# First blocks of S rearranged: block 0 loaded in column halves, its x tile alone, and the low halves of blocks 1 and 2 made in front of the next block's sums

## The reference

```python
x = x + gnn(layernorm(x), adj, adj)      # x [2048, 512], adj [2048, 2048]
x = x + ffn(layernorm(x)[None], ...)[0]

def gnn(x, Coefficient2, A):             # called with Coefficient2 = A = adj
    S = (A + A.T) * 0.5 + eye
    deg = S.sum(1); dinv = where(deg > 0, deg ** -0.5, 0)
    return (Coefficient2 @ (dinv[:, None] * S * dinv[None, :])) @ x
# ffn: 8 routed experts (top 1) and a shared one, weights made ternary
```

## Time and profile before

| | us |
|---|---|
| median of 3 runs (727.76 to 730.76) | 729.55 |
| the profiled execution | 729.79 |
| its span in the profile | 728.1 |
| PE busy | 659.4 |
| DVE busy | 488.8 |
| ACT busy | 390.1 |
| POOL busy | 202.4 |
| PE's first matmul of the stage | 19.25 |
| last matmul of block 15 starts | 112.67 |

### The profile page before, as it was taken

How to read it: one execution, slowest core, us unless ns; L and a number is a source line. 1 busy time by engine, 2 the same in 40 slices (tenths; PEclk the granted TensorE clock), 3 DMA queues, 4 the chain that set the end, 5 groups by cost and what they waited for, 6 DMA issues and landing times.

```text
span 728.1 us, 16147 instructions
## 1 busy us (share of the span) xinstructions
PE 659.4 (91%) x5313; PEld 385.2 (53%) x5313; DVE 488.8 (67%) x1071; ACT 390.1 (54%) x726; POOL 202.4 (28%) x195
## 2 busy tenths in 40 slices
PE   0799998999998999999868788799999999999995
PEld 0344443444444554444424365477767676777763
DVE  4878966646674556589899868966775465555554
ACT  2667547859986765777547662223342233233331
POOL 2123310000000000077666606620020445344332
PEclk9999999999999999999998999999999999999999
DMA  8999942675887787667566785354248677677751
GB/s 350 416 420 417 417 172 58 193 185 144 228 243 243 256 271 269 234 207 226 173 240 215 226 228 147 92 164 105 86 59 203 147 211 186 179 191 176 174 148 34
DMA packets 107103, 151.68 MB, mean 208 GB/s; under 512 B 64286, under 2 KB 64286, under 8 KB 102944
## 3 DMA queue, kind: packets, MB, share of 16 engines
q1 hardware_dynamic: 91280, 117.74, 52.5%
q0 software_dynamic: 6960, 20.99, 9.7%
q10 hardware_dynamic: 8800, 12.09, 5.2%
HBM read 119.57 MB, written 19.16 MB: 191 GB/s over the span
## 4 chain that ended last, share of the span: by engine, by line
PE 60%; DVE 13%; DMA 10%; issue 7%; POOL 4%; ACT 4%; DVEq 0%; SPq 0%; ACTq 0%; POOLq 0%
PE bank L1536 14%; PE bank L1509 14%; PE bank L1375 9%; PE bank L1377 9%; PE bank L1376 9%; DMA region<-in_adj_t 5%; DMA work<-in_w 2%; PE bank L1414 2%; DVE work L1081 2%; POOL xb L578 2%; DVE xb L1127 1%; POOL xb L580 1%; ACT junk L732 1%; DVE s L1062 1%; DMA work<-in_adj_t 1%
## 5 line engine op out<-in xcount | busy, mean ns | idle before, releaser
L1536 PE MATMUL bank<-region,work 128*128 (+1 forms) x624 | 142.5, 382 | 4.2 <-DVE work L1229 4.2
L870 ACT ACTIVATE work<-work 128x512 f32<-128x512 f32 x78 | 48.5, 622 | 180.6 <-DVE work L1219 180.6
L1375 PE MATMUL bank<-zreg,work 128*128 (+1 forms) x256 | 98.2, 384 | 13.6 <-DVE work L1150 10.8
L1509 PE MATMUL bank<-zreg,region 128*128 128x128 f16 x1728 | 100.9, 219 | 0.0
L1509 PEld LDWEIGHTS bank<-zreg,region 128*128 (+1 forms) x1728 | 98.1, 98 | 4.3
L1376 PE MATMUL bank<-zreg,work 128*128 (+1 forms) x256 | 98.1, 383 | 0.0
L1377 PE MATMUL bank<-zreg,work 128*128 (+1 forms) x256 | 98.1, 383 | 0.0
L1536 PEld LDWEIGHTS bank<-region,work 128*128 128x128 f16 x624 | 59.2, 98 | 70.8 <-issue 8.9
L1375 PE MATMUL bank<-region,work 128*128 128x512 f16 (+1 forms) x192 | 74.8, 389 | 23.1 <-DVE region L994 23.1
L732 ACT ACTIVATE junk<-work 128x512 f16<-128x512 f32 x124 | 77.7, 626 | 22.8 <-DMA work<-in_w 20.7
L575 POOL TENSOR_TENSOR rb<-rb,power 128x2 f32<-128x2 f32 x16 | 17.4, 1087 | 255.5 <-DVE rb L1141 255.4
(11 more groups left out here) (158 smaller groups left out, 1009.8 us busy)
## 6 DMA issues: line engine op xcount, KB each, us to landing
work<-in_w SPq DMA_DIRECT2D x62, 512.0 KB, 4.1
region<-in_adj SPq DMA_DIRECT2D x16, 1024.0 KB, 10.8
region<-in_adj_t SPq DMA_DIRECT2D x16, 1024.0 KB, 7.5
work<-in_adj_t SPq DMA_DIRECT2D x32, 384.0 KB, 4.2
zreg<-s_scratch SPq DMA_DIRECT2D x24, 256.0 KB
xb<-in_w SPq DMA_DIRECT2D x10, 512.0 KB, 4.2
zreg<-in_x SPq DMA_DIRECT2D x4, 1024.0 KB, 9.8
h_scratch<-hb POOLq DMA_DIRECT2D x16, 256.0 KB, 3.7
```

Of the source, the lines that this page charges most:

```text
L870: nc.scalar.activation(h1[:, cols], pre[:, cols], ACT.Silu).then_inc(h1_ok, 1)
L1375: nc.tensor.matmul(dst, a_hi, b_hi, start=start, stop=False, skip_group_check=True)
L1509: last = nc.tensor.matmul(ps_h[b][f // 4][:, (f % 4) * P:(f % 4 + 1) * P], w, ht[n % RING][:, c:c + P], start=(f % 4 == 0 and d == 0 and h ...
L1536: last = nc.tensor.matmul(ps_y[b][:, :].rearrange("p (d c) -> p d c", d=DB), h1hl[:, b, h, f * P:(f + 1) * P], w, start=(f == 0 and h == 0 ...
```

## The change

Block 0's two loads are split into column halves with semaphores of their own, so that the sums of the first 1024 columns wait for the first halves alone. Tile 0 of x is a load of its own in front of block 1; tiles 1 to 3 (`x_rest`) follow block 1. In every round the next x batch is loaded one block later. On DVE the statistics, the root and the scales of tile 0 are made by themselves, the low half of S's block 0 comes in front of them, and for blocks 1 and 2 low_s, dinv_of and low_u come in front of the next block's sums. On ACT the moments of batch 1 move by one step: none after block 0.

```diff
-            load_a(0, 0, True)
-            sp.dma_start(xhat[:, 0:UNROLL, :], x_t[:, 0:UNROLL, :]).then_inc(x_in[0], 16)
+            for c in (slice(0, G0_COLS), slice(G0_COLS, N)):
+                half = first_half if c.start == 0 else first_rest
+                sp.dma_start(a_in[:, 0, c], adj_j[0, :, c]).then_inc(half, 16)
+                sp.dma_start(t_in[:, 0, c], adjt_j[0, :, c]).then_inc(half, 16)
+            sp.dma_start(xhat[:, 0:1, :], x_t[:, 0:1, :]).then_inc(x_in[0], 16)
...
             load_a(1, 1, True)
+            sp.dma_start(xhat[:, 1:UNROLL, :], x_t[:, 1:UNROLL, :]).then_inc(x_rest, 16)
+            load_a(2, 2, True)
             load_x(1)
-            for s in range(2, UNROLL):
-                load_a(s, s, True)
+            load_a(3, 3, True)
             with sp.Fori(1, NT // UNROLL - 1) as i:
                 for s in range(UNROLL):
                     load_a(UNROLL * i + s, s, False)
-                    if s == 0:
+                    if s == 1:
                         load_x(i + 1)
...
             AFTER = {0: (0, 1, 2), 1: (3,), 2: (4, 5)}
+            AFTER_FIRST = {1: (0, 1), 2: (2, 3, 4, 5)}
...
-            sums_of(0, 0)
-            dve.wait_ge(x_in[0], 16)
-            for s in range(UNROLL):
-                x_stats(0, s)
-            x_first()
-            dinv_of(0, 0)
-            x_scales(0, True)
-            stream_round(0, False)
+            one, others = slice(0, 1), slice(1, UNROLL)
+            sums_of(0, 0)
+            dve.wait_ge(x_in[0], 16)
+            x_stats(0, 0)
+            x_first(0, one)
+            low_s(0, 0)
+            dinv_of(0, 0)
+            x_first_scales(0, one)
+            dve.wait_ge(x_rest, 16)
+            x_stats(0, 1)
+            low_u(0)
+            for s in range(2, UNROLL):
+                x_stats(0, s)
+            x_first(1, others)
+            sums_of(1, 1)
+            x_first_scales(1, others)
+            for s in range(1, UNROLL - 1):
+                low_s(s, s)
+                dinv_of(s, s % 2)
+                low_u(s)
+                sums_of(s + 1, s + 1)
+            x_mean(1)
+            dinv_of(UNROLL - 1, 1)
+            stream_step(0, UNROLL - 1, False)
+            x_scales(1)
```

More of the change, by code:

```diff
@@ L231, in build @@
         rest_ok = sem("rest_ok")
+        first_half = sem("first_half")
+        first_rest = sem("first_rest")
+        x_rest = sem("x_rest")
         shi_ok = sem("shi_ok")
@@ L554, in x_root, with x_first_root @@
             def x_root(batch):
-                pool.wait_ge(xv_ok, batch + 1)
+                pool.wait_ge(xv_ok, batch + 2)
                 nc.gpsimd.tensor_tensor(r4[:, 1, :], r4[:, 0, :], power[:, :], ALU.pow).then_inc(xr_ok, 1)
+            def x_first_root(part, c):
+                pool.wait_ge(xv_ok, part + 1)
+                nc.gpsimd.tensor_tensor(r4[:, 1, c], r4[:, 0, c], power[:, c], ALU.pow).then_inc(xr_ok, 1)
             def degree_root(j, b):
@@ L699, in stream_round @@
                     if not last:
-                        for k in AFTER.get(s, ()):
+                        for k in (AFTER if i else AFTER_FIRST).get(s, ()):
                             x_moment(i + 1, k)
@@ L949, in x_var, with x_scales @@
                 nc.vector.tensor_scalar(r4[:, 0, :], xsum[:, 1, :], 1.0 / D, EPS, ALU.mult, ALU.add).then_inc(xv_ok, 1)
[L951 to L955, removed]
+            def x_scales(batch):
+                dve.wait_ge(xr_ok, batch + 2)
+                dve.wait_ge(nm_ok, batch + 2)
+                dve.wait_ge(xn_ok, UNROLL * batch)
                 nc.vector.tensor_scalar(r4[:, 2, :], r4[:, 1, :], U_SCALE, None, ALU.mult)
@@ L962, in sums_of @@
                 b = s % 2
-                dve.wait_ge(a_loaded[s], 4 * (j - s) + 16)
-                dve.wait_ge(t_loaded[b], 8 * (j - b) + 16)
+                opening = isinstance(j, int) and j == 0
+                if opening:
+                    dve.wait_ge(first_half, 32)
+                else:
+                    dve.wait_ge(a_loaded[s], 4 * (j - s) + (16 if s else 0))
+                    dve.wait_ge(t_loaded[b], 8 * (j - b) + (16 if b else 0))
                 nc.vector.scalar_tensor_tensor(out=a_in[:, s, 0:G0_COLS], in0=a_in[:, s, 0:G0_COLS], scalar=1.0,
@@ L968, in sums_of @@
                                                accum_out=rs[:, b, 0:1]).then_inc(sum_ok, 1)
+                if opening:
+                    dve.wait_ge(first_rest, 32)
                 halves = lambda v: v.rearrange("p (g n) -> p g n", g=2)
@@ L996, in lows, with stream_step @@
                                                op1=ALU.subtract).then_inc(ulo_ok, 1)
+            def stream_step(i, s, last):
+                j = UNROLL * i + s
+                more = s < UNROLL - 1 or not last
+                if more:
+                    sums_of(j + 1, (s + 1) % UNROLL)
+                if not last and s == 2:
+                    x_mean(i + 1)
+                if not last and s == 3:
+                    x_var(i + 1)
+                low_s(j, s)
+                low_u(j)
+                if more:
+                    dinv_of(j + 1, (s + 1) % 2)
@@ L998, in stream_round @@
             def stream_round(i, last):
                 for s in range(UNROLL):
[L1000 to L1014, removed]
+                    stream_step(i, s, last)
                 if not last:
-                    x_scales(i + 1, False)
+                    x_scales(i + 1)
+            one, others = slice(0, 1), slice(1, UNROLL)
             sums_of(0, 0)
             dve.wait_ge(x_in[0], 16)
-            for s in range(UNROLL):
-                x_stats(0, s)
```

23 lines of the change are left out of this document (15 added, 8 removed).

## The result

The changed kernel takes 734.9 us in the median of 22 runs, against 729.5 of the kernel before on the same chip: a ratio of 1.0065, interval 1.0045 to 1.0085, or 4.7 us (3.3 to 6.2). It is slower, and the median lies beyond the range's upper end of 732.7. (The two medians lie 5.4 us apart; the 4.7 is what the ratio gives, and the text goes by it.) The profiled execution took 732.7 us with a span of 731.0, 2.9 us above that of before.

The account below looks back on a forecast made before the run. PE, busy 659.4 of 728.1 us, bounds the kernel; the stage's end hangs on block 5, waiting for t6 in a full load stream. 729.79 - 1.25 + 1.25 + 1.1 = 730.9, less 0.24: 730.7 us, range 727.8 to 732.7.

Parts of the forecast that it names:

- the opening: Block 0's loads and first statistics: sums start at 6.0, second halves there at 8.54, PE starts at 18.0.
- - 1.25 (PE's start): Term for PE's first matmul: it starts at 18.0, 1.25 us earlier.
- which waits for t6: Block 5 waits for block 6's transposed load as before, starts at 52.66 and gives back 1.25 us.
- t6's sums more than 0.5 us from 47.9: Sign that the prediction is wrong: DVE's sums of block 6 start over 0.5 us away from 47.9.
- rival 4: Small loads: three added loads each pay 2.5 us, t6 7.5 us later, kernel at 737; chance 0.07.
- It decides from about 1.2 us a load: Added cost per small load on the stream from which the slower-by-more-than-0.5 % outcome would hold.
- Blocks 1 to 3: Ready at 26.15, 32.2 and 41.9 to 42.3; three PE gaps become one of 4.5 to 4.9 us before block 3.
- The clock: A half-speed stretch of 3.41 us on blocks 3 and 4: 1.4 lost, less 0.3 slack, +1.1.
- The queue: SP issues t5 at 34.45 instead of 31.27; the load pipe is empty 0 to 0.6 us, covered by the clock drop.
- Rival 1: Block 3 late and the clock drop on the path: 730.7, own range 729.9 to 731.6; chance 0.48.
- Rival 2: Clock drop falls into the wait, block 5 starts at 52.7 to 53.2: 729.5 to 730.0; chance 0.24.
- Rival 3: Loads come sooner and PE's earlier start passes through: 728.3; chance 0.16.

Follow-up runs that it names:

- piece kernel: The order kernel with each of block 0's two loads one transfer of 4 KB half-row pieces, first sums waiting for all: ratio 1.0043.
- order kernel: The changed kernel with block 0 loaded whole again (two 1 MB loads); lone tile 0 of x and new DVE order stay: ratio 1.0025.
- second profile: The changed kernel run again, unaltered, in a second series: ratio 1.0041 against the kernel before, mark 72.77.
- kernel with neither: The changed kernel with block 0 loaded whole and the old order of the low halves; tile 0 of x alone and later x batches stay: ratio 0.9975.
- low halves alone: The kernel before with only DVE's order changed, low halves of blocks 1 and 2 before the next sums; loads and x tiles as before: ratio 1.0015.

## Why the prediction was wrong

**The failed step is the opening**: "First halves: the bytes of one load instead of two, so the sums start at 8.54 - 2.56 = 6.0 ... Second halves: 8.54". It took the stream as a pipe whose time goes by bytes. At its head it doesn't: four transfers of 512 KB are complete at 10.19 to 10.40 where two of 1 MB are at 8.34 to 8.64, and from 2 to 6 us the halves move 232 to 244 GB/s where whole loads move 342 to 354. The piece kernel shows that the smaller pieces are up to a third of it and the number of transfers the rest; the kernel with blocks 0 to 3 in halves shows that it is the head of the queue that is dear. Why the head is slow is not shown. So the term "- 1.25 (PE's start)" measured +0.59, and with it fell the term beside it, a block 5 "which waits for t6" at 47.92: t6's sums start at 50.61 and 52.47. That is the prediction's own sign of being wrong, "t6's sums more than 0.5 us from 47.9".

This is **rival 4**, slower by small loads, which had a chance of 0.07. Its mechanism was right and its size wrong: priced at 2.5 us for each of three loads (t6 7.5 us late, 737), it measured 1.5 us at t6 in all (49.44 and 49.33 against 47.92). By its own measure of 1.2 us a load it would not have decided; that the result falls into its part of the forecast takes the other costs below. The evidence against it, 512 KB pieces at 385 GB/s, was of a queue long in flow and not of one that starts. The Trainium skill, DMA: Bandwidth & Descriptors, Anatomy of one DMA, gives the fixed 2.0 us a transfer, and it does so for transfers issued by GpSimd, where these are issued by SP. The two halves more at the head cost less than 1 us each and those in the full queue less than 0.1, so the measurements bear out its direction and not its size as an unhidden cost.

**"It decides from about 1.2 us a load"** was wrong with it: that took the halves' cost as adding only to t6. It adds to PE's chain too.

**Blocks 1 to 3** were right. The order kernel has block 1 at 26.18 (forecast 26.15), block 2 at 32.25 (32.2) and block 3 at 42.26 (41.9 to 42.3). At block 3 two small errors cancel, which is luck: there the row of sums up to `x_mean` takes 3.22 us (32.11 to 35.33), with a wait of 0.54 in it, and not 2.80, and from `x_mean` to L990 it is 4.59 and not 5.0. (The four, not five, small operations that DVE has more, 1075 instructions against 1071, do not matter here.) In the changed kernel the same steps run from a start 2.06 us later: 44.30 - 19.84 = 24.46 there, 42.26 - 17.78 = 24.48 here. A block's DVE work takes 34.16 - 28.10 = 6.06 us in the new order, against 5.18 of PE, with 0.44 of waiting for POOL's root and 0.79 for ACT's high half in it: DVE stands in these waits, which the old order filled with sums. "Turns three gaps into one" holds too, and the kernel with block 3 in the new order shows that the gap then only moves.

**The clock.** "I take 1.4 lost, less 0.3 of slack: +1.1" was too small: the order kernel loses half of 3.41, 1.7, and has 0.04 of slack (block 3 at 42.26 + 10.36 = 52.62, against 52.66): +1.64. That is a term mis-sized by 0.5. Without the drop the mark there would not have been back at 0: t6's sums start at 48.69, which allows block 5 at 53.44, so the drop is worth 0.9 beyond the data. In the changed kernel the stretch was 6.83 once and 3.41 once. That it is the place that costs, and not the drop, shows in the halves with the old order: there the clock is 0.50 from 30 to 36 us, behind a gap of 3.71 in front of block 1, and block 5 still starts at 54.08, 4.75 behind t6's sums, as the data allow.

**The queue.** "The pipe is empty for 0 to 0.6 us. With the clock drop this is covered" is half right. It is the order that makes the hole. SP's issue of t5 was forecast for 34.45 and came at 34.51 in the order kernel; there t6 is 0.77 late and PE, slowed by the clock, does not see it. The rate from 36 to 42 us is 361 GB/s there, against 404 to 422 in the kernels with the old order. With the late opening t5 is issued at 36.56, the rate falls to 309 to 331 GB/s, and t6 comes at 50.6 to 52.5. So on the data's side too the parts add up to more than their sum: +0.77 by the order, +1.4 to 1.5 by the halves, +2.7 to +4.6 by both.

**The sum in measured terms**, on PE's chain in the first profile: block 3 starts at 42.26 in the order kernel and 2.04 later with the halves, 44.30; two blocks 10.36; the clock 2.63: 57.29, against 52.66 before. (In the second profile the clock costs 1.7 and 0.9 more go by until t6's data release block 5 at 57.22. Nothing in the two profiles ties these two ends to each other, so that the marks are nearly the same is put down to chance.) So +4.6 = 1.6 (order, clock within it) + 2.0 (the late opening, all of it) + 1.0 (the longer half-speed stretch, or t6's lateness). Before, the late opening would have met slack in front of blocks 4 and 5, and cost only its 1.5 on the data; the new order had used that slack up. That is why the two parts cost more together than apart.

**The other rivals.** Rival 1 had the gap, the clock and the place right and describes the kernel without the halves. Rival 2, the drop hidden in the wait in front of block 3, is refuted: in the order kernel the whole stretch (42.60 to 46.01) lay on PE's work, which had begun at 42.26, and in the changed one 5.35 us of 6.83 did. (In the second profile of the changed kernel the drop was hidden after all, but in t6's lateness and not in that wait.) Rival 3, the gain kept, is refuted for the stage: "the gain of the opening is gone by block 5" is shown by the kernel with neither, which starts 1.40 earlier and reaches block 5 0.21 earlier.

## What to carry to other kernels

Splitting the first loads so that work may start sooner is to be tested by itself, since the rate of a queue's first transfers is not that of the stream: here two transfers more delayed the whole stream by 1.5 us and the first complete block by 1.7 to 2.0. When work is moved ahead on an in-order engine, count what it then waits for: here the roots and high halves of other engines, hidden before, made 6 us of a block and gathered three small gaps into one long one. And two costs that each fit into a slack are not both free: write the chains that meet at the next wait one beside the other, with each one's slack, and add on each.

## What was not expected of the hardware

- One kernel gave half-speed stretches of 6.83 and of 3.41 us behind the same gap (4.64 and 4.65 us idle), and t6's arrival at 50.61 and 52.47, with nearly the same mark.
- A half-speed stretch followed a gap of 2.61 us in the kernel before, and none followed a gap of 2.72 us in the kernel with the low halves alone. What tells these two apart is open.
- In block 0 the matmuls start 0.43 us apart and not 0.216, for 2.9 us in the kernel before and 5.9 in the changed one, though the granted clock is listed as 1.00 there. It costs the stage nothing, since block 1 starts when its data release it: at 28.23 with that stretch of 5.9 us, and at 28.16 in the second profile, where the stretch was 3.8.
- The head of the queue: 201 to 258 GB/s from 4 to 6 us with halved loads, where whole loads have 385 to 418; 178 from 2 to 4 us with 4 KB pieces, where whole loads have 274 to 299; and 401 with halved loads in a full queue.
